# Attention sums fetched packed by head, reciprocals made during attention, two output tiles

## The reference

```python
qkv = layer_norm(x, g1, be1) @ w_qkv                   # 8 heads of 16
scores = einsum('nhd,mhd->hnm', q, k) * 16 ** -0.5
attn = softmax(where(adj != 0, scores, -inf), axis=-1)
out = einsum('hnm,mhd->nhd', attn, v).reshape(n, 128)
x = x + out @ w_proj + b_proj
x = x + gelu(layer_norm(x, g2, be2) @ w1 + b1) @ w2 + b2          # 128 -> 512 -> 128
h = x @ Wt.T + bt                                      # 64 wide
s = leaky_relu(h @ Wa.T + ba, 0.2)                     # one number for each row
w = softmax(where(adj > 0, s, -9e15), axis=1)          # s is the same along a row
y = x + (w @ h) @ Wp.T + bp
out = layer_norm(y) * gamma + beta
```

## Time and profile before

| what | value |
|---|---|
| time, median of 3 runs | 1263.87 us (1261.6 to 2189.83) |
| time of the profiled execution | 1264.83 us |
| its span, first to last instruction | 1263.1 us |
| mean granted clock of PE, share of full | 0.987 |
| busy in the span: PE, DVE, ACT, POOL | 1168.2, 1119.6, 1060.4, 968.0 us |
| moved by DMA | 194.40 MB, 154 GB/s on average |

### The profile page before, as it was taken

The page is one execution under the profiler, slowest core; times in us unless marked ns, Lnnn a source line. Parts: engine busy times, 40 slices in busy tenths (PEclk is TensorE's granted clock), DMA queues, the critical chain, the costliest instruction groups (busy, mean ns, idle before and its releaser), DMA issues. The chain is left out here.

```text
span 1263.1 us, 31456 instructions
## 1 busy us (share of the span) xinstructions
PE 1168.2 (92%) x11628; PEld 331.8 (26%) x11639; DVE 1119.6 (89%) x1622; ACT 1060.4 (84%) x1218; POOL 968.0 (77%) x1010
## 2 busy tenths in 40 slices
PE   5888899999999999999999899999999988999986
PEld 2222221111111121111111111111111126775433
DVE  6988889999999999999999899999999974665856
ACT  5999999999999999999999899999999973441000
POOL 5677779999999999999998788888888852543322
PEclk9999999999999999999999999999999988999988
DMA  4333336555444554555445445555554357505971
GB/s 165 105 117 93 118 84 207 153 160 146 159 135 140 163 151 149 152 166 154 135 134 175 127 140 145 170 154 153 150 163 135 102 180 260 186 26 219 352 303 29
DMA packets 52671, 194.40 MB, mean 154 GB/s; under 512 B 6496, under 2 KB 20640, under 8 KB 42272
## 3 DMA queue, kind: packets, MB, share of 16 engines
q1 hardware_dynamic: 38944, 156.65, 34.9%
q0 software_dynamic: 9216, 33.56, 13.0%
q10 hardware_dynamic: 4352, 2.10, 0.6%
HBM read 114.69 MB, written 44.04 MB: 126 GB/s over the span
## 5 line engine op out<-in xcount | busy, mean ns | idle before, releaser
L1402 DVE SCALAR_TENSOR_TENSOR probs<-m,ps 128x512 f32<-128x512 bf16 (+1 forms) x1024 | 926.2, 950 | 34.0 <-PE ps L1593 17.4
L1295 ACT ACTIVATE probs<-probs 128x1536 f32<-128x1536 f32 x512 | 847.7, 1656 | 0.9
L1184 POOL TENSOR_TENSOR probs<-probs,m 128x512 f32<-128x512 f32 x512 | 621.9, 1226 | 130.2 <-ACT probs L1289 97.9
L1608 PE MATMUL ps<-probs,v_sb 128*17 128x512 f32 x4096 | 540.3, 600 | 0.0
L1593 PE MATMUL ps<-kq 32*128 32x512 bf16 x6144 | 423.9, 378 | 55.1 <-DVE probs L1402 23.3
L1289 ACT ACTIVATE probs<-ps 128x512 f32<-128x512 f32 x512 | 391.7, 765 | 9.2 <-PE ps L1593 8.3
L1593 PEld LDWEIGHTS ps<-kq 32*128 32x128 bf16 x6144 | 116.3, 92 | 568.8 <-ACT probs L1289 430.3
L1177 POOL TENSOR_SCALAR m<-adj_in 128x512 bf16<-128x512 int32 x256 | 181.3, 708 | 0.2
L1608 PEld LDWEIGHTS ps<-probs,v_sb 128*17 128x17 f32 x4096 | 68.2, 95 | 217.7 <-issue 208.3
L454 ACT ACTIVATE probs<-ps 128x512 f32<-128x512 f32 x8 | 4.8, 597 | 83.5 <-PE ps L799 81.5
L377 POOL TENSOR_TENSOR v_sb<-v_sb,cols 128x4 f32<-128x4 f32 (+1 forms) x9 | 8.8, 976 | 71.7 <-DVE v_sb L650 71.7
(11 more groups left out here) (142 smaller groups left out, 624.1 us busy)
## 6 DMA issues: line engine op xcount, KB each, us to landing
adj_in<-in_adj_t SPq DMA_DIRECT2D x64, 1024.0 KB, 5.9
mask_t<-m SPq DMA_DIRECT2D x64, 512.0 KB, 2.9
counts<-m POOLq DMA_DIRECT2D x64, 512.0 KB, 4.6
kq<-mask_t SPq DMA_DIRECT2D x16, 2048.0 KB, 9.7
counts_t<-counts SPq DMA_DIRECT2D x8, 512.0 KB, 7.5
attn_t<-acc_sb SPq DMA_DIRECT2D x16, 256.0 KB, 6.6
adj_in<-attn_t SPq DMA_DIRECT2D x8, 512.0 KB, 4.0
v_sb<-counts_t SPq DMA_DIRECT2D x8, 512.0 KB, 7.0
```

The costliest lines, as they stand in the source:

```text
L1184: nc.gpsimd.tensor_tensor(pr, pr, m01[:, (k // 2) % MRING, :], ALU.mult).then_inc(postmasked, 1)
L1295: nc.scalar.activation(pr, pr, ACT.Exp, scale=UNIT).then_inc(exped, 1)
L1402: nc.vector.scalar_tensor_tensor(out=pr, in0=m.to_broadcast([P, n, CH]), scalar=1.0, in1=ps[:, b:b + n, :], op0=ALU.subtract, op1=ALU.add)\
L1608: last = nc.tensor.matmul(ps[RT * hh:RT * hh + VW, 6 + g, :], v_sb[:, t, h * VW:(h + 1) * VW], probs[:, k % SLOTS, hh // 2, (hh % 2) * CH: ...
```

## The change

Sums of exponentials: after a chunk's sums have been stored, SP fetches the 17th row of each head in 8 small transfers into a tile of 128 partitions by 32 words, `head_sums` (16 partitions for a head); DVE takes one reciprocal over it (`invert`), and SP stores the result in DRAM (`inv_dram`). For chunks 0 to 6 this stands in the attention loops, in groups with G % 8 = 2 and 4 on SP and at k % 64 = 24 on DVE. For chunk 7 it stands in the tail, the reciprocal in iteration 2 of DVE's dense loop.

`load_sums` now makes four transfers: the 16 rows of each head, packed to 64 partitions, for each of the two groups; the reciprocals, each row repeated for the 16 partitions of its head; and x. `normalise_att` is one multiplication on DVE of two 128 x 512 tiles in SBUF into one of two `attT` tiles. `turn_acc`, `turn_att` and ACT's `turned_att` are gone. `x1` and `x1b` have two buffers. PE's order in the dense loop becomes `project(i + 1)`, the four parts of `ff1(i)`, `turn_x2(i - 1)`, `ff2(i)`, `turn_h2(i + 1)`, `hidden(i - 1)`. The first chunk's projection stands between `products(509)` and `products(510)`. SP asks for the first mask half after chunk 7's sums have been stored and its row sums asked for; the other four of the first five stand later among the loads of the sums. `y_out` has two buffers with a semaphore each, so `finish(j)` waits for the store of chunk j - 2.

```diff
         def load_sums(sp, c):
             if c >= 2:
-                sp.wait_ge(acc_turned, c - 1)
+                sp.wait_ge(attT_made, c - 1)
                 sp.wait_ge(xb_made, c - 1)
-            sp.dma_start(acc[c % 2][:, :, :], a_dram[c, :, :, :]).then_inc(acc_in[c % 2], 16)
+            for g in range(2):
+                rows_of = a_dram[c, :, g, :].rearrange("(h r) n -> h r n", r=RT)
+                sp.dma_start(outs[c % 2][g * HG * HD:(g + 1) * HG * HD, 0, :], rows_of[:, 0:HD, :])\
+                    .then_inc(acc_in[c % 2], 16)
+            sp.dma_start(outs[c % 2][:, 1, :], inv_dram[c].rearrange("h (a n) -> h a n", a=1).to_broadcast([H, HD, CH]))\
+                .then_inc(acc_in[c % 2], 16)
             ...
+        def load_head_sums(sp, c):
+            sp.wait_ge(acc_stored, 32 * (c + 1))
+            if c > 0:
+                sp.wait_ge(inverse_stored, 16 * c)
+            for g in range(2):
+                rows_of = a_dram[c % NC, :, g, :].rearrange("(h r) (s n) -> h r s n", r=RT, s=HD)
+                for hh in range(HG):
+                    at = (g * HG + hh) * HD
+                    sp.dma_start(head_sums[at:at + HD, :], rows_of[hh, HD, :, :]).then_inc(sums_in, 16)
+
+        def store_inverse(sp, c):
+            sp.wait_ge(inverted, c + 1)
+            sp.dma_start(inv_dram[c % NC].rearrange("h (s n) -> (h s) n", s=HD), head_sums[:, :])\
+                .then_inc(inverse_stored, 16)
+
+        def invert(dve, c):
+            dve.wait_ge(sums_in, 16 * H * (c + 1))
+            nc.vector.reciprocal(head_sums[:, :], head_sums[:, :]).then_inc(inverted, 1)
...
-            sp.wait_ge(acc_stored, 32 * (NC * R - 1))
+            sp.wait_ge(inverse_stored, 16 * (NC * R - 1))
             load_sums(sp, 0)
             load_sums(sp, 1)
-            sp.wait_ge(scored, TLS * R)
-            load_edges(sp, 0)
             for g in range(2):
                 sp.wait_ge(acc_copied[g], NC * R)
                 sp.dma_start(a_dram[NC - 1, :, g, :], acc_sb[:, g, :]).then_inc(acc_stored, 16)
             load_sums(sp, 2)
+            load_head_sums(sp, NC * R - 1)
+            sp.wait_ge(scored, TLS * R)
+            load_edges(sp, 0)
+            load_sums(sp, 3)
             load_edges(sp, 1)
-            for n in range(2, ERING):
-                load_sums(sp, n + 1)
-                load_edges(sp, n)
-            for c in range(ERING + 1, NC):
-                if c == NC - 1:
-                    sp.wait_ge(acc_stored, 32 * NC * R)
-                load_sums(sp, c)
+            load_sums(sp, 4)
+            store_inverse(sp, NC * R - 1)
+            load_sums(sp, 5)
+            load_edges(sp, 2)
+            load_sums(sp, 6)
+            load_edges(sp, 3)
+            sp.wait_ge(inverse_stored, 16 * NC * R)
+            load_sums(sp, NC - 1)
+            load_edges(sp, 4)
...
             def normalise_att(c):
-                ...
+                dve.wait_ge(acc_in[c % 2], LOADED * (c // 2 + 1))
+                if c >= 2:
+                    dve.wait_ge(projected, c - 1)
+                nc.vector.tensor_tensor(attT[c % 2], outs[c % 2][:, 0, :], outs[c % 2][:, 1, :], ALU.mult)\
+                    .then_inc(attT_made, 1)
...
             for i in range(NC):
+                if i + 1 < NC:
+                    first_sum(i + 1)
                 if i >= 2:
                     hidden_low(i - 2)
                 if i + 1 < NC:
-                    first_sum(i + 1)
                     normalise_x1(i + 1)
-                second_sum(i)
                 if i + 2 < NC:
                     normalise_att(i + 2)
+                if i == 2:
+                    invert(dve, NC * R - 1)
+                second_sum(i)
...
-                if j > 0:
-                    dve.wait_ge(out_stored, 32 * j)
+                if j > 1:
+                    dve.wait_ge(out_stored[j % 2], 32 * (j // 2))
...
             products(TLS * R - 4)
-            turn_acc(0)
             products(TLS * R - 3)
+            project(0)
             products(TLS * R - 2)
-            turn_att(0)
             products(TLS * R - 1)
-            project(0)
             ...
-            turn_acc(1)
             turn_h2(0)
             for i in range(NC):
-                ff1(i, (0, 1))
-                if i + 1 < NC:
-                    turn_att(i + 1)
-                ff1(i, (2, 3))
                 if i + 1 < NC:
                     project(i + 1)
+                ff1(i, (0, 1, 2, 3))
                 if i >= 1:
                     turn_x2(i - 1)
                 ff2(i)
-                if i + 2 < NC:
-                    turn_acc(i + 2)
                 if i + 1 < NC:
                     turn_h2(i + 1)
```

More of the change, by code:

```diff
@@ L185, in gnn_kernel @@
         b_sb, s_sb = wb(CH), wb(CH)
-        x2c, y, y_out = wb(SUB, D), wb(SUB, D), wb(SUB, D)
+        x2c, y, y_out = wb(SUB, D), wb(SUB, D), [wb(SUB, D), wb(SUB, D)]
         csT, csum_w = wb(P), wb(D)
@@ L308, in tail_sync @@
                     load_counts(sp, n // 2)
-            sp.wait_ge(out_stored, 32 * NC)
+            for u in range(2):
+                sp.wait_ge(out_stored[u], 16 * NC)
         def tail_gpsimd(pool, R):
@@ L360, in tail_gpsimd @@
                     input_bias(i + 2)
+                x2_bias(i)
                 if i >= 1:
@@ L658, in finish @@
                 dve.wait_ge(yr_made, n + 1)
-                if j > 0:
-                    dve.wait_ge(out_stored, 32 * j)
+                if j > 1:
+                    dve.wait_ge(out_stored[j % 2], 32 * (j // 2))
                 for s in range(at.start, at.stop):
-                    last = nc.vector.scalar_tensor_tensor(out=y_out[:, s, :], in0=y[:, s, :], scalar=yrs[:, s:s + 1],
+                    last = nc.vector.scalar_tensor_tensor(out=y_out[j % 2][:, s, :], in0=y[:, s, :], scalar=yrs[:, s:s + 1],
                                                           in1=beta_r, op0=ALU.mult, op1=ALU.add)
@@ L683, in tail_tensor @@
             pe.wait_ge(tail_in, N_TAIL_IN)
-            def turn_acc(c):
-                pe.wait_ge(acc_in[c % 2], 32 * (c // 2) + 32)
-                if c >= 1:
-                    pe.wait_ge(att_made, c)
-                else:
-                    pe.wait_ge(opened, TLS * R)
-                    pe.wait_ge(premasked, 2 * TLS * R)
-                for g in range(2):
-                    for s in range(SUB):
-                        last = nc.tensor.transpose(ps[:, B_ACC + g, s * P:(s + 1) * P],
-                                                   acc[c % 2][:, g, s * P:(s + 1) * P], identf[:, :])
-                last.then_inc(acc_turned, 1)
-            def turn_att(c):
-                pe.wait_ge(att_made, c + 1)
-                if c >= 1:
-                    pe.wait_ge(h2T_made, c)
-                for s in range(SUB):
-                    last = nc.tensor.transpose(ps[:, B_TURN, s * P:(s + 1) * P],
-                                               att[:, s * H:(s + 1) * H, :].rearrange("p h d -> p (h d)"),
-                                               identf[:, :])
-                last.then_inc(att_turned, 1)
             def project(c):
@@ L1065, in _ @@
                     store_acc(G // per_chunk - 1)
+                if G >= per_chunk and G % per_chunk == 2:
+                    load_head_sums(sp, G // per_chunk - 1)
+                if G >= per_chunk and G % per_chunk == 4:
+                    store_inverse(sp, G // per_chunk - 1)
             def second(sp):
@@ L1069, in second @@
                 store_acc(NC - 1)
-                sp.wait_ge(acc_stored, 32 * NC)
+                load_head_sums(sp, NC - 1)
+                store_inverse(sp, NC - 1)
+                sp.wait_ge(inverse_stored, 16 * NC)
                 sp.wait_ge(tail_in, N_TAIL_IN)
@@ L1086, in second @@
                         store_acc(G // per_chunk - 1)
+                    if G >= GROUPS + per_chunk and G % per_chunk == 2:
+                        load_head_sums(sp, G // per_chunk - 1)
+                    if G >= GROUPS + per_chunk and G % per_chunk == 4:
+                        store_inverse(sp, G // per_chunk - 1)
             def tail(sp, R):
@@ L1414, in masks @@
             def masks(k, begin):
+                if k >= begin + 2 * NT and k % (2 * NT) == 24:
+                    invert(dve, k // (2 * NT) - 1)
                 pre_mask(k, 1, 1)
@@ L1476, in second @@
                     copy_acc(NC - 1, g)
+                invert(dve, NC - 1)
                 all_reach(dve, phase)
```

77 lines of the change are left out of this document (28 added, 49 removed).

## The result

| what | before | after |
|---|---|---|
| median | 1264.46 us (6 runs; 1257.68 to 1266.86, and one of 2189.83) | 1258.38 us (6 runs; 1255.79 to 1260.44) |
| profiled execution, its span | 1264.83, 1263.1 us | 1259.27, 1257.5 us |
| busy: PE, DVE, ACT, POOL | 1168.2, 1119.6, 1060.4, 968.0 us | 1158.5, 1126.7, 1056.0, 968.8 us |

The ratio after to before is 0.995 (95% interval 0.993 to 0.997). So 6 us came where 12.8 were forecast. The time lies in the range and outside what was called the forecast's own (1247 to 1255). One of the two stretches that were to win did win its sum. The other lost part of its gain, and two losses stand ahead of it and behind it.

The account below looks back on a forecast made before the run. ACT bounds attention, PE the dense stage, and the edge stage PE's rhythm plus a store stall. Gains of 4.5 (dense, start 0) and 8.3 (output tiles) make 12.8: 1252.0 us profiled, 1251.1 median; range 1246 to 1260.

Parts of the forecast that it names:

- the forecast's own: The main case, chance 0.57: 1247 to 1255 us, covering the start's bounds and the reciprocals' 2.4 us.
- the two stretches that were to win: Dense stage, 4.5 us from shorter periods, and edge stage, 8.3 us from two output tiles.
- The start: Start of the tail: later data and less PE work cancel, `ff2(0)` at 1058; gain 0, between +1.4 and -2.1.
- the 12 fewer transposes: Start of the tail: less PE work before the last product was to cancel the later data of x.
- The dense stage: Periods between `ff2`: middle five gain 0.46 us each, first 1.6, last 0.6; together 4.5 us.
- the 0.1 for a refill: Middle dense periods: 0.1 us added for PE's refill after idle time, making 10.76 us.
- Two output tiles: Edge stage: `finish(3)` no longer waits for store 2, `project_sums` keeps its 11.90 us rhythm; gain 8.27 us.
- The rival that DMA is full without the pause: Edge stage, chance 0.2: stores stay in flight too long and PE still loses time; 1253.5 to 1259.4 us.
- Reciprocals in attention: Attention, chunks 0 to 6: seven DVE reciprocals of 0.346 us; cost taken as 0, 2.4 us kept for the range.
- The slower rival: Attention, chance 0.06: DVE's `invert` waits for row sums and stalls ACT 7 times; 1275 us, or 1303.
- The port: Start of the tail: DVE's SBUF multiplication waits 1.2 us because POOL's `input_bias` starts first and holds the port.
- Masks later: Mask halves asked for later, about 1051 to 1090, still about 40 us before use: cost 0.

Follow-up runs that it names:

- both edits: Changed kernel with the last products and DVE's copies ahead of `project(0)`, and the last chunk's reciprocal in iteration 0: 1251.76 us, ratio 0.9885.

## Why the prediction was half right

**The start, forecast at 0, cost 3.1 us** in the profiled pair. (The three executions with the old order take 26.4 to 29.5 us from the last pair to `ff2(0)`, the four with the changed start 30.4 to 30.8; the means differ by 2.7.) This is the step that failed. "Now data comes at about 1037": the sum took the two more transfers for two more issues, and priced them by SP's 0.4 to 0.8 us each. The issues did cost that: from the first load's to x's it is 1.93 us, before 0.47. (SP also reached the first load 0.7 us later after ACT's last pair than before; in the changed kernel's second execution it did not.) But the data came at 1043.5, 3.5 us later by the flight alone, 8.5 us for 5.0, since what was asked for ahead of x is cut by head into outer dimensions of 4 and 8. The row that priced the flight, 5 us, was that of plain transfers of 128 rows. With the same bytes in plain rows it is 5.7, packed by feature 4.9. The second half of the step failed with it: the 12 fewer transposes were to cancel the later data, but `products(510)` and `(511)` are behind the projection and so behind the data. Ahead of it they are free (27.5 us to `ff2(0)` against 30.8).

**The dense stage: right, but for one period.** Forecast 9.9, five times 10.76, 9.9; the undisturbed ones are 9.81, 10.46, 9.81, with the 0.34 us of idleness for ACT's gelu (L428) that the earlier trace rows gave. The middle ones are 0.3 us shorter than forecast, 1.2 us in four: from `ff1` to `ff2` it is 4.57 us (1088.95 to 1093.52) for the 4.73 taken from the last chunk, and the 0.1 for a refill did not show. (The 3.67 us in the sums for the first and the last period stands in no row shown; the 9.9 made with it came out at 9.81.) The 12.82 us took back 2.1 against the forecast's 10.76. The prediction named the place ("SP now stands at `store_inverse` until iteration 2 of DVE; behind it wait chunk 5's sums") and priced it at 0, counting one chunk's load against one period. This is the second step that failed, a wait put at nothing. It did not count the whole queue behind: 19.6 us of standing, then three chunks' loads in one bunch with the mask halves, of which the one ahead of chunk 7's loads holds SP for 6.6 us, and 18.7 us until chunk 7's x is there. With the reciprocals made in iteration 0 the period is 10.46. Net -3.9 for -4.5.

**Two output tiles: right.** 8.27 in the profile, 7.8 and 8.1 in the medians of two jobs. The rival that DMA is full without the pause did not come: no store is waited for.

**Reciprocals in attention: right, 0.** From chunk 0's copy of its sums to ACT's last pair it is 832.4 us, before 832.7. The slower rival (DVE blocked in `invert`) did not come: no idleness at L277. The 1.8 us by which attention ends later are not theirs: two output tiles alone have no reciprocals there and end at 1032.63. They come in the first 40 us: a step of ACT that starts at 40.38 before starts at 42.38 after. Granted clock there, before, then after:

```profile
20.00:40.00 20.00, 16.27 (x144) 5.67 (x136) 18.52 (x31) 17.51 (x24) 14.46 (x18) 0.91 0.38 137
```

```profile
20.00:40.00 20.00, 17.70 (x128) 6.49 (x120) 16.32 (x29) 15.72 (x21) 13.39 (x17) 0.79 0.34 119
```

Before and "both edits" have 0.91 there and end attention at 1030.19 and 1030.30; the other eleven executions have 0.77 to 0.84 and end it between 1030.75 and 1032.76, and the two of "two output tiles alone" stand at 1032.63 and 1030.75. So it is scatter of an execution, which a median of several runs lessens.

**The port.** The 1.2 us that DVE was to wait did not come. DVE was issued first and took its 0.69; POOL's addition is the one that grew, 1.69 us against 1.27. The Trainium skill's rule (SBUF — State Buffer, "Who interferes with whom") is that the one that issues first holds the port; the trace agrees, with the roles exchanged from what was assumed. The 1.69 stands beside PE's projection and costs nothing.

**Masks later: right, 0** for the masks themselves; none is waited for in the edge stage.

**A half clock that nothing in the sum had.** Behind PE's 2.75 us of idleness at 1173.80 the step of the edge stage is 13.3 to 13.6 us in nine of the ten profiled executions of kernels with the new dense order, and 11.9 in the tenth (the changed kernel's second, with the same 2.74 us of idleness) and in all three with the old order (one of them with 2.74 too). So it is mostly, not always, a cost of the change, 1.7 us. Why the new order brings it is open: no run changed this place alone.

So the gains of the 12.8 us exist. Missing are 3.1 (start), 0.6 (dense, net), 1.7 (half clock), and in the profiled pair 1.8 of attention's scatter, which the medians hold in part only: 6.1 us there. What the change does beside the output tiles is worth +3.1 - 3.9 + 1.7 = +0.9 by the profile, and nothing by the medians.

## What to carry to other kernels

A transfer is priced by its form, not by its bytes and its issue: look for the row of a transfer with the same outer dimension before taking a flight time, and order data so that what is fetched late has many rows outermost. When a wait is put on an engine's queue, list all that stands behind it up to the next point that matters, with the time that the bunch takes to be issued, not only the first item. And what is ready goes ahead of what waits for a transfer, on PE above all: two products and two copies cost 3.4 us of the start only because of their place.

## What the runs showed of the hardware

The instruction that issues a transfer can itself hold its queue: 2 MB halves took SP 0.42 and 0.51 us at 1057.25 and 1089.46, 2.89 at 1060.09, and 6.62 and 7.56 us at 1092.47 and 1103.23, behind a bunch of others. A small transfer can be held as well: with the reciprocals in iteration 0 the issue of their store, 16 KB, took 8.56 us at 1066.95, where the changed kernel's took 0.33.

Transfers of the same bytes differ by their form: x behind them landed after 8.1 us (sums by head, outer dimension 4; 7.9 to 8.5 in six executions), 5.7 (128 plain rows) and 4.9 (outer dimension 16), one execution each. The old loads, plain too, took 4.8 to 6.3 in three.

The same idleness of PE, 2.74 or 2.75 us, was followed by half clock in one execution of the changed kernel and not in the other (5.30 and 3.62 us for the same matmuls). And the granted clock from 20 to 40 us was anywhere from 0.77 to 0.91; the end of attention moved by up to 2.6 us with it, though not in strict order (0.83 ended at 1030.75, 0.84 at 1032.39).
